# Up products of a routed expert group on 192 columns where its group leaves the last 64 of 256 empty, chosen by a branch per expert

## The reference, cut to what matters

```
logits = xf @ Wg                      # 2048 x 256 by 256 x 8
idx = argmax(logits)                  # one of 8 experts for each token
for e in range(8):                    # W1, W2: 256 x 1024, W3: 1024 x 256
    y = (gelu(xf @ W1[e]) * (xf @ W2[e])) @ W3[e]
    final += where(idx == e, y, 0)
out = h + shared + final
```

## Time and profile before

| | us |
|---|---|
| median of 3 runs | 485.52 (484.78 to 487.93) |
| the profiled execution | 484.74 |
| its span, first to last instruction | 483.0 |
| PE busy / weight loads busy in the span | 476.5 / 426.8 |
| DVE busy / ACT busy | 330.0 / 247.4 |
| granted TensorE clock | 1.00 (2.4 GHz) |

### The profile page before, as it was taken

The page is one execution under the profiler, slowest core; times in us unless marked ns, Lnnn a source line. Parts: engine busy times, 40 slices in busy tenths (PEclk is TensorE's granted clock), DMA queues, the critical chain, the costliest instruction groups (busy, mean ns, idle before and its releaser), DMA issues.

```text
span 483.0 us, 8526 instructions
## 1 busy us (share of the span) xinstructions
PE 476.5 (99%) x3052; PEld 426.8 (88%) x3053; DVE 330.0 (68%) x541; ACT 247.4 (51%) x376; POOL 82.3 (17%) x92
## 2 busy tenths in 40 slices
PE   8999999999999999999999899999999999999997
PEld 7998888889888888888888899889999998999887
DVE  2659668678686887767744677647775776677564
ACT  3766774575663464443433656236555563655321
POOL 4431031011011010103360002100201021011460
PEclk9999999999999999999999999999999999999999
DMA  5952121001210002100454445504553466241292
GB/s 158 357 156 85 34 76 56 33 23 57 60 62 1 1 0 103 74 0 29 146 175 73 173 157 202 190 24 158 188 191 142 167 208 217 98 154 56 55 334 92
DMA packets 25543, 55.12 MB, mean 114 GB/s; under 512 B 7264, under 2 KB 18784, under 8 KB 21536
## 3 DMA queue, kind: packets, MB, share of 16 engines
q1 hardware_dynamic: 19184, 43.32, 26.7%
q0 software_dynamic: 2976, 8.14, 5.1%
q10 hardware_dynamic: 3344, 3.15, 2.2%
HBM read 42.25 MB, written 12.35 MB: 113 GB/s over the span
## 4 chain that ended last, share of the span: by engine, by line
PE 94%; DVE 3%; issue 1%; ACT 1%; DVEq 0%
PE ps L280 26%; PE ps L281 25%; PE ps L282 25%; PE ps L799 6%; PE ps L801 3%; PE ps L505 2%; PE ps L829 2%; PE ps L831 1%; PE ps L613 1%; PE ps L660 1%; PE ps L648 1%; PE ps L820 1%; PE ps L695 1%; DVE stats L1290 1%; PE ps L673 0%
## 5 line engine op out<-in xcount | busy, mean ns | idle before, releaser
L280 PE MATMUL ps<-xW,w_slots 128*128 128x256 f32 x256 | 73.6, 288 | 1.5 <-issue 1.4
L282 PE MATMUL ps<-xW,w_slots 128*128 128x256 f32 x256 | 72.4, 283 | 0.0
L281 PE MATMUL ps<-xW,w_slots 128*128 128x256 f32 x256 | 72.4, 283 | 0.0
L1225 DVE TENSOR_TENSOR hT<-ps,hT 128x512 fp32r<-128x512 f32 x64 | 43.9, 686 | 35.6 <-ACT hT L963 18.7
L482 POOL DMA_INDIRECT y_tokens<-y_rows,to_rows x30 | 36.0, 1200 | 181.5 <-DVE y_rows L1616 171.8
L1596 DVE TENSOR_TENSOR w_slots<-stage,w_slots 128x2048 fp32r<-128x2048 f32 x24 | 54.8, 2285 | 2.8 <-ACT w_slots L1111 2.8
L280 PEld LDWEIGHTS ps<-xW,w_slots 128*128 128x128 f32 x256 | 48.7, 190 | 2.5 <-issue 1.6
L281 PEld LDWEIGHTS ps<-xW,w_slots 128*128 128x128 f32 x256 | 48.8, 191 | 0.0
L282 PEld LDWEIGHTS ps<-xW,w_slots 128*128 128x128 f32 x256 | 48.7, 190 | 0.0
L974 ACT ACTIVATE hT<-ps 128x512 fp32r<-128x512 f32 x32 | 19.1, 597 | 53.8 <-DVE ps L1231 53.8
L799 PE MATMUL ps<-w_slots,hW 128*128 128x512 f32 x128 | 46.6, 401 | 0.0
(11 more groups left out here) (209 smaller groups left out, 1276.0 us busy)
## 6 DMA issues: line engine op xcount, KB each, us to landing
stage<-ew_in SPq DMA_DIRECT2D x24, 1024.0 KB, 4.9
x_sorted<-zero_row SPq DMA_DIRECT2D x32, 128.5 KB, 2.6
stage<-w1s_in SPq DMA_DIRECT2D x2, 1024.0 KB, 8.2
fetched<-y_tokens SPq DMA_DIRECT2D x4, 512.0 KB, 6.7
x_pair<-x_sorted ACTq DMA_DIRECT2D x7, 256.0 KB, 2.6
out_rows<-fetched SPq DMA_DIRECT2D x3, 512.0 KB, 3.0
first_stage<-tok_w_in SPq DMA_DIRECT2D x1, 1024.0 KB, 4.8
first_stage<-tok_w_in SPq DMA_DIRECT2D x4, 256.0 KB, 4.5
```

The source lines that it names most:

```text
L280: pe.matmul(dst, lhs_hi, rhs_hi, start=start, stop=False, skip_group_check=shares_bank)
L281: pe.matmul(dst, lhs_hi, rhs_lo, start=False, stop=False, skip_group_check=shares_bank)
L282: return pe.matmul(dst, lhs_lo, rhs_hi, start=False, stop=stop, skip_group_check=shares_bank)
L1225: dve.tensor_tensor(hT[:, c % RING, 1, :], ps[:, bank, :], f32(hT[:, c % RING, 0, :]), ALU.subtract).then_inc(h_lo, 1)
```

## The change

DVE makes a flag per expert in `place_singles`: `held` is the expert's tokens less 128 for each of its singles, that is, the rows of its window that hold a token, and the flag is 1 where `held` is at most 192. The flags are a further piece of `turns`. The rows of a window stand in order, so that the rows from 192 on hold no token there.

PE reads the flag of each expert once, ahead of up 0, and each of the four up steps becomes an `If`: with the flag, 24 products on 192 columns; without, the 24 products on 256 columns as before. The work of ACT and DVE on the banks stays at 256 columns for each chunk; where columns 192 to 255 weren't written, it works on what lay in the bank. `window_down` is the same.

By the counts above, `held` is 144, 240, 188, 241, 209, 200, 165 and 149: the flag is 1 for experts 0, 2, 6 and 7 and 0 for experts 1, 3, 4 and 5.

```diff
     WINDOW = 2 * P
+    FEW = WINDOW - P // 2
...
+        held = small("held", [P, EXPERTS])
...
+        def fewer_of(engine, e):
+
+            return engine.value_load(turns[0:1, bass.ds(e + FEWER, 1)], min_val=0, max_val=1)
...
-            def window_up(e, p, odd):
+            def window_up(e, p, odd, rows=WINDOW):
...
-                            last = mm3(pe, ps[:, p % 2 * 2 + w, c * WINDOW:(c + 1) * WINDOW], w_slots[:, o:o + P],
-                                       w_slots[:, o + PART:o + PART + P], xW[:, odd, 0, k, :], xW[:, odd, 1, k, :],
+                            last = mm3(pe, ps[:, p % 2 * 2 + w, c * WINDOW:c * WINDOW + rows], w_slots[:, o:o + P],
+                                       w_slots[:, o + PART:o + PART + P], xW[:, odd, 0, k, 0:rows], xW[:, odd, 1, k, 0:rows],
                                        k == 0, k == KD - 1)
                     last.then_inc(done, 1)
+
+            def window_up_of(fewer, e, p, odd):
+
+                with pe.If(fewer > 0):
+                    window_up(e, p, odd, FEW)
+                with pe.Else():
+                    window_up(e, p, odd)
...
+                fewer = fewer_of(pe, e)
                 pe.wait_ge(pair_lo, e + 1)
...
-                window_up(e, 3, odd)
+                window_up_of(fewer, e, 3, odd)
...
+                step(dve.scalar_tensor_tensor(out=held[:], in0=singles[:], scalar=-float(P), in1=counts[:], op0=ALU.mult,
+                                              op1=ALU.add))
+                step(dve.tensor_scalar(turns[:, FEWER:FEWER + EXPERTS], held[:], float(FEW), None, ALU.is_le))
```

More of the change, by code:

```diff
@@ L47, in build @@
     TOTAL = ROWS + EXPERTS + 1
+    FEWER = TOTAL + 1
     SPLITS = EXPERTS + 2
@@ L216, in build @@
         pos = small("pos", [P, TILES], I32)
-        turns = small("turns", [P, TOTAL + 1], U16)
+        turns = small("turns", [P, FEWER + EXPERTS], U16)
         x_one = small("x_one", [P, D])
         singles = small("singles", [P, EXPERTS])
+        held = small("held", [P, EXPERTS])
         singles_upto = small("singles_upto", [P, EXPERTS])
@@ L863, in expert @@
                 pe.wait_ge(split_lo, e * 3 + 5)
-                window_up(e, 0, odd)
+                window_up_of(fewer, e, 0, odd)
                 if opening:
@@ L887, in expert @@
                     single_turn(last_of(pe, e), 0)
-                window_up(e, 1, odd)
+                window_up_of(fewer, e, 1, odd)
                 with pe.If(count > 0):
@@ L891, in expert @@
                 pe.wait_ge(w_lo, e * PAIRS + 1)
-                window_up(e, 2, odd)
+                window_up_of(fewer, e, 2, odd)
                 if not (isinstance(e, int) and e == EXPERTS - 1):
```

## The result

The changed kernel takes **490.80 us** (median of 20 runs, 486.48 to 497.39), the kernel before 486.26 us on the same chip (20 runs, 484.78 to 488.37). The ratio is 1.0075, with a 95% interval of 1.0054 to 1.0096: slower by 2.6 to 4.7 us, where 482.2 us was forecast. The profiled execution took 492.2 us, 7.5 more than that of before, so the two traces show the loss larger than the medians do. The ratio leaves out the three longest executions of the changed kernel (493.94, 495.39 and 497.39 us); the medians take in all.

What follows compares the result with a forecast made beforehand. PE's unbroken instruction stream was taken to bound the kernel: 484.74 − 3.8 (products) + 0.4 (branches) = 481.3 us, or 482.1 against the median of the runs, stated as 482.2; range 475.4 to 487.5 us.

Steps and rivals of the forecast that it cites:

- branches: Compare-and-branch at 32 up steps plus each expert's flag load: 0 for experts 1 to 7, 0.4 us at expert 0.
- Products: 384 up products on 192 columns in place of 256: 0.110 us each instead of 0.120, saving 3.8 us.
- Rival 1: Only columns count in the 384 narrower up products: 0.027 us saved each, 475.6 us, 2% faster; chance 12%.
- 0.024 us of the earlier trace: Pace read from sixteen products of 128 columns with 32-column loads; taken to show narrow products can be quick with small loads.
- constant of 0.013 us: Part of an up product's 0.120 us beside the 0.107 us of its 256 columns; might come on top of the load.
- Rival 3: Float32r up products of 192 columns take a slower two-pass form, 0.173 us each: 20 us more, 505.9 us; chance 10%.
- The loop fetched again: PE's expert loop no longer stays held, so two back-edges wait for a fetch, some 1.4 us each, 2.8 us.
- rival 2: In the up steps, nothing to gain, or branches or refetched code eat the gain: 484 to 487 us; chance 20%.
- branches eat it: PE's sequencer sets the pace, so each branch costs: 0.1 us for each of 32 steps, 3.2 us, all the gain.
- Rival 4: Stalls: most of the 32 branches at up steps cost over 0.27 us; at 0.5, 12 us more, 498 us; chance 4%.
- Flags: Two small DVE steps beside `place_singles`, about 0.17 us each, under PE's shared-expert products: 0; without that cover 0.4 us.
- Waits on DVE: In up steps 2 and 3 the wait for `w_lo` sits on the branch, 1.0 us left at step 3: covered, 0.

Runs made afterwards that it cites:

- short code: PE's code for a third and later single of an expert left out: changed kernel 484.41 us (ratio 0.9966), kernel before 484.41 us (0.9962).
- flags moved: The changed kernel with its two flag steps moved three chunks later on DVE: 492.02 us, ratio 1.0096.
- 224 with the long code: The changed kernel with limit and short product at 224 rows in place of 192, code equally long: 490.77 us, ratio 1.0062.
- the flags alone: The kernel before with only the two small DVE steps that compute the flags, which nobody reads: 486.95 us, ratio 1.001.
- the last version: The changed kernel at 224 rows, expert 0 without a branch, code for further singles as in the kernel before: 484.96 us, ratio 0.9957.

## Why the prediction was wrong

**The step that failed** is the price of the longer code. Under *branches* the prediction said: "The new jumps pass over 24 products only, and I take 0 for experts 1 to 7", and 0.4 us for expert 0. It priced instructions that PE executes. What costs is code that PE must be given: four further arms in each copy of the expert, some 200 instructions. The profiled execution lost 4.99 + 0.48 us at expert 1, for which 0 was forecast, and 0.74 + 1.63 at expert 0, for which 0.4 was (there 0.74 is within what unchanged PE code shows). With the short code the change took 484.41 us, 0.0109 of the time less than with the long. The cue stood in the earlier trace rows, a gap of 1.36 us at a jump that skips the singles. It was put down to an emptied instruction queue and a long jump; it is a block of code on its way (a packet that ended 1.55 us ahead of PE's restart), and each expert has such a jump.

Point by point:
- *Products:* forecast 0.110 us, measured 0.111, and the gain of 3.4 us for 3.8. Right, and for the reason given: 128, 192 and 224 columns take the same. On this the Trainium skill, "TensorE: Matmul & The Clock Gate", section "LDWEIGHTS (loading the stationary operand)", gives columns / 1.2 ns, 107 for 128 columns; the trace lies 4 ns above it. The prediction set a second rule against this one, and wrongly: the Trainium skill, in the same text, section "Back-to-back issue gap", gives N / 2.4 + 2.5 ns for an isolated product and says that in a stream of loads and products both set the spacing. Rival 1 (columns alone) is out. Two readings on the way were wrong, and the result doesn't hang on them. The 0.024 us of the earlier trace rows is no pace of one product behind another: at 0.42 ns a column 128 columns need 0.053, and the source puts these products at four column positions of the array in turn (`tile_position`). And that the constant of 0.013 us is the same at 256 and 512 columns, rival 1's support, is no finding, since it was worked out from just these two.
- *Rival 3* (a slower form of float32r below 256) is out by the same rows.
- *The loop fetched again,* in rival 2: false for the changed kernel (27 packets, the number forecast), true for it with 64 more dead products (36) and for the kernel with dead code in every expert (45). 27 packets, taken as a sign that the code does no harm, show only that nothing was fetched twice, not that each came in time. The Trainium skill, "Runtime: NRT & Kernel Launch", section "Instruction fetch mechanics", says that a taken branch to code that isn't held forces a fetch, and that crossing into the next block is mostly hidden. The first agrees with the earlier trace rows and its gap of 1.36 us; to the second this case has an exception, the stall of 3.74 us, ten products into straight code.
- *Rival 2's "branches eat it"* came nearest in size (484 to 487) but not in mechanism: 32 compares with short code cost nothing (0.987 with, 0.9884 without), nor do 28 compares with their jumps. *Rival 4* (stalls of over 0.27 us at most branches) had the right sign for a wrong reason: two places, not most of 32.
- *Flags:* forecast 0, measured 0 to 1.6 us.
- *Waits on DVE:* 0 was forecast. From up 2 to up 3 experts 2 and 6 take 4.98 us in place of 4.69, waiting for `gTp`; the versions at 192 columns without a stall at expert 1 have it too, so this 0.6 us is a cost of the shorter steps that the sum lacked. PE also waited 0.8 us for `hW` at expert 7; the two other traces with a stall above 3.7 us at expert 1 (flags moved, 224 with the long code) have it too, 0.7 and 1.0, and the versions with short code don't. That the stall causes it was not tested.
- *The clock* stood in no term. It fell behind both stalls of the changed kernel (2.1 and 3.7 us) and, in other versions, with waits of 1.7 to 6.7 us; it stayed full behind 2.5 us with the flags alone, 2.1 in the last version and 3.5 at expert 0 with dead code everywhere. So the length of the wait doesn't decide it alone. Nor is it peculiar to the change: of the 111 executions of the kernel before in the experiments 39 have a mean clock of 0.996 or 0.997, and their median is 488.4 us, that of the others 486.1.

**What stays open.** Why a block arrives in time in one layout and not in another isn't shown from inside. The runs show that length and place of never executed code matter, that the same code in the same place stalls for 1.2 to 4.6 us, and that at expert 1 the packet travelled beside a weight transfer on all engines. Whether it started late because of that transfer, or because PE asked late, isn't known; moving the transfer wasn't tried.

## What to carry to other kernels

On an engine that is never idle, a second arm is not free because it is not run: price added code by the blocks that the engine must fetch and by the jumps over them, and test it by adding dead code of that length to the kernel before. Before narrowing a product, see what paces it: with a 128-column load, nothing below 256 columns was worth anything beyond the first 0.009 us, so choose the widest limit that has that pace (224 rather than 192, for two more experts at the same price). If a change shows its saving and the time doesn't fall, sum up the waits by "issue" and look at the clock and at the packets of the instruction queue beside each.

## What the runs showed that was not expected

- Dead code alone made a kernel 6% slower (515.57 us), and a shift of all code behind expert 0's singles by 64 or 128 instructions moved another by −3.5 or +4.3 us between medians (−2.3 or +4.2 by the ratios).
- From the end of a packet on the instruction queue to PE's next product it took 1.1 to 2.0 us, in 37 of PE's 38 waits on "issue".
- Waits of 1.7 to 6.7 us on PE came often, not always, with some 3 us at half the clock, which cost 1.6 us on a step of 24 products, near as much as the wait.
- A turn of a loop with an `If` that isn't entered cost PE 0.55 us.
